# A three-batch GNN pipeline: every state and the neighbour sums take their turn through device memory, and the first norm moves

## The reference, cut to what matters

```python
adj_norm = adj / (jnp.sum(adj, axis=-1, keepdims=True) + EPS)
h_neigh = jnp.einsum('bnm,bmf->bnf', adj_norm, x)
h = relu(jnp.einsum('bnk,ko->bno', concat([x, h_neigh]), weight) + bias)
x = _layernorm(x + h)
...
A = (adj != 0).astype(x.dtype); h = x
for l in range(5):
    m = jnp.einsum('bnd,de->bne', h, weight[l])
    agg = jnp.einsum('bij,bid->bjd', A, m)
    h = _gru_cell(agg, h, w_ih, w_hh, b_ih, b_hh)
x = _layernorm(x + h * mask)
```

## Time and profile before

| what | value |
| --- | --- |
| median of 3 runs | 609.56 us (608.76 to 610.24) |
| the profiled execution, its own time | 608.95 us |
| its span, first to last instruction | 606.9 us |
| busy: TensorE, VectorE, ScalarE, GpSimd | 589.7, 513.5, 419.4, 419.4 us |
| mean granted TensorE clock | 0.992 |
| DMA: moved, share of the 16 engines | 73.55 MB, 37.7% |

### The profile page before, as it was taken

The page is one execution under the profiler, slowest core; times in us unless marked ns, Lnnn a source line. Parts: engine busy times, 40 slices in busy tenths (PEclk is TensorE's granted clock), DMA queues, the critical chain, the costliest instruction groups (busy, mean ns, idle before and its releaser), DMA issues.

```text
span 606.9 us, 9921 instructions
## 1 busy us (share of the span) xinstructions
PE 589.7 (97%) x2733; PEld 479.4 (79%) x2733; DVE 513.5 (85%) x1151; ACT 419.4 (69%) x777; POOL 419.4 (69%) x335
## 2 busy tenths in 40 slices
PE   7999999999999999999999999999999999999992
PEld 6678788888888888888888888888888888877771
DVE  5986969898998989899898989989898898966677
ACT  5767685958778595876868587685867768555451
POOL 0645464878868687886869688687977868755343
PEclk9999999999999999999999999999999999999996
DMA  8713122454344446334444534445453433010101
GB/s 271 294 35 114 54 76 88 134 180 121 123 151 112 161 127 190 121 121 146 115 154 138 190 112 130 141 115 158 138 174 110 148 138 95 10 53 10 44 0 53
DMA packets 74002, 73.55 MB, mean 121 GB/s; under 512 B 5760, under 2 KB 49280, under 8 KB 73984
## 3 DMA queue, kind: packets, MB, share of 16 engines
q1 hardware_dynamic: 73712, 73.20, 37.7%
q10 hardware_dynamic: 272, 0.13, 0.1%
HBM read 56.00 MB, written 17.30 MB: 121 GB/s over the span
## 4 chain that ended last, share of the span: by engine, by line
PE 91%; DVE 4%; DMA 1%; issue 1%; ACT 1%; SPq 1%; POOL 0%; POOLq 0%; DVEq 0%
PE ps_tok L1405 12%; PE ps_tok L1412 12%; PE ps_r L1269 6%; PE ps_r L1270 6%; PE ps_r L1271 6%; PE ps_z L1269 6%; PE ps_z L1271 6%; PE ps_z L1270 6%; PE ps_b L1271 3%; PE ps_b L1269 3%; PE ps_b L1270 3%; PE ps_in L1270 3%; PE ps_in L1271 3%; PE ps_hn L1271 3%; PE ps_in L1269 3%; PE ps_hn L1270 3%
## 5 line engine op out<-in xcount | busy, mean ns | idle before, releaser
L686 POOL TENSOR_TENSOR z_h<-z_gate,h 128x512 f32<-128x512 f32 x80 | 110.2, 1377 | 24.1 <-ACT z_gate L893 24.0
L676 POOL TENSOR_TENSOR h_lo<-h,h_hi 128x512 fp32r<-128x512 f32 x64 | 88.5, 1383 | 53.8 <-ACT h_hi L708 53.8
L811 ACT ACTIVATE ps_in<-ps_in,gru_bias 128x512 f32<-128x512 f32 x80 | 52.8, 660 | 53.6 <-DVE ps_in L1132 53.5
L1405 PE MATMUL ps_tok<-edges,tok_hi 128*128 (+1 forms) x320 | 87.8, 396 | 0.7 <-ACT tok_hi L708 0.7
L1412 PE MATMUL ps_tok<-edges,tok_lo 128*128 (+1 forms) x320 | 87.6, 396 | 0.0
L1248 DVE SCALAR_TENSOR_TENSOR r_hn<-ps_hn,gru_bias,r_gate 128x512 f32<-128x512 f32 x80 | 59.6, 745 | 28.1 <-ACT r_gate L883 26.9
L615 POOL TENSOR_TENSOR adjt_lo<-adjt_in,adjt_hi 128x512 fp32r<-128x512 f32 x56 | 72.1, 1312 | 4.3 <-ACT adjt_hi L708 4.3
L1405 PEld LDWEIGHTS ps_tok<-edges,tok_hi 128*128 128x128 f32 x320 | 59.7, 188 | 15.6 <-ACT tok_hi L708 0.9
L1412 PEld LDWEIGHTS ps_tok<-edges,tok_lo 128*128 128x128 f32 x320 | 59.9, 188 | 14.7 <-DVE tok_lo L919 0.3
L883 ACT ACTIVATE r_gate<-ps_r,rz_bias 128x512 f32<-128x512 f32 x80 | 55.2, 691 | 20.0 <-PE ps_r L1271 17.0
L1173 DVE SCALAR_TENSOR_TENSOR ps_in<-z_gate,ps_in 128x512 f32<-128x512 f32 x80 | 55.1, 689 | 10.9 <-ACT ps_in L811 8.6
(11 more groups left out here) (156 smaller groups left out, 1599.0 us busy)
## 6 DMA issues: line engine op xcount, KB each, us to landing
adjt_in<-in_adj_t_dram SPq DMA_DIRECT2D x14, 1024.0 KB, 5.4
adj_in<-in_adj_dram SPq DMA_DIRECT2D x14, 1024.0 KB, 5.3
rows<-passage SPq DMA_DIRECT2D x144, 64.0 KB, 2.0
passage<-early_blocks SPq DMA_DIRECT2D x24, 256.0 KB, 2.1
x_in<-in_x_dram SPq DMA_DIRECT2D x16, 256.0 KB, 3.8
xt_in<-in_x_t_dram SPq DMA_DIRECT2D x15, 256.0 KB, 3.0
out_dram<-y_out SPq DMA_DIRECT2D x15, 256.0 KB, 2.3
passage<-last_blocks SPq DMA_DIRECT2D x14, 256.0 KB, 2.1
```

The costliest lines, as they stand in the source:

```text
L676: nc.gpsimd.tensor_tensor(h_lo[new][:], h[new][:], raw(h_hi[new][:]), ALU.subtract).then_inc(s_h_lo, 1)
L686: nc.gpsimd.tensor_tensor(z_h[:], z_gate[:], h[own][:], ALU.mult).then_inc(s_zh, 1)
L1405: nc.tensor.matmul(ps_tok[:], tok_hi[:, c * P:(c + 1) * P], edges_from(c, unit[0]), start=c == 0, stop=False)
```

## The change

- **MOVED** takes slot 4 as well: state 3 goes through device memory (new `passage3`, `rows3`), and the TensorE turn between slots 3 and 4 goes.
- **Neighbour sums.** For windows 2 to 14 (`means`), VectorE transposes the 32x32 blocks of `ps_b[2]` in slot 1 into `late_blocks`, SyncE stores them to `mean_passage` and loads `mean_rows` with 4 DMAs. ScalarE's copy to `mean_t` and TensorE's turn in slot 2 go. `mean_parts` runs in slot 3 and adds into the banks `ps_b[0]` and `ps_b[1]`, where the products `own` now stay.
- **SyncE's queue.** Store 1, store means, load 1, load means, store 3, load 3, and then the adjacency loads.
- **Edges** are made in slot 0 and no longer in slot 2. The last batch's statistics move to slot 2.
- **First norm.** Residual and statistics in slot 3, moments in slot 4 ahead of `agg_lo`, and `norm1` behind `agg_lo`; `x1` is turned on TensorE between the z gate and the in gate of slot 4 (before: ahead of the r gate).
- **GpSimd** makes `tok_lo` for slot 4 (before: VectorE), and in slot 4 runs `z_h` ahead of the two `h_lo`.
- **Layer 0's state products** in the moved windows run their `h_lo` parts last (`first_state_products`), which wait for `s_h0_lo` alone.
- **ScalarE**: `xt_hi` goes from slot 0 to slot 4 of the window before, `x_kept` from slot 4 to slot 3; the scratch output of the row sums is `r_gate`.
- The wait for `s_agg_lo` stands directly ahead of the gates in every slot.

```diff
-MOVED = {slot: UNITS[slot][1] for slot in (1, 2, 3)}
+MOVED = {slot: UNITS[slot][1] for slot in (1, 2, 3, 4)}
...
+    def means(self):
+        return self.prepares() and not self.ramps()
...
                     store_state(w, 1)
+                if w.means():
+                    store_blocks(late_blocks, mean_passage, s_nsum_out, w.prepared(1, 1), s_mean_passed)
+                if w.trips():
                     load_state(w, 1)
+                if w.means():
+                    load_rows(mean_rows, mean_passage, s_mean_passed, w.passed(16, 1), s_mean_rows)
+                if w.trips():
+                    store_state(w, 3)
+                    load_state(w, 3)
...
-                        if slot == 2 and not w.ramps():
-                            if w.first >= 3:
-                                dve.wait_ge(s_agg, w.last_layers())
-                            edge_half(0)
+                        if slot == 2 and not w.ramps() and w.finishes():
+                            stats2_of_batch()
...
                         if slot == 0 and w.makes_parts():
+                            if not w.ramps():
+                                dve.wait_ge(s_adj_in, w.prepared(16, 16))
+                                if w.first >= 3:
+                                    dve.wait_ge(s_agg, w.last_layers())
+                                edge_half(0)
                             xw_parts(0)
+                            if not w.ramps():
+                                edge_half(1)
...
+                            if w.means():
+                                dve.wait_ge(s_nsum, w.prepared(1, 1))
+                                nc.vector.transpose(late_blocks[:]..., ps_b[2][:]...).then_inc(s_nsum_out, 1)
...
-                        if slot == 4 and not w.ramps():
-                            norm1(w)
+                        if w.means() and slot == 4:
+                            moments1(w)
...
-                        if slot == 2 and not w.leads():
+                        if slot == 2 and w.first == 1:
                             sums_by_tokens(w.prepared(1, 1))
...
-                    if unit:
+                    if unit and layer == 0 and w.first > 2:
+                        first_state_products()
+                    elif unit:
                         state_products(slot)
...
                         gate(ps_z, 1, agg_hi, agg_lo, wi_hi, wi_lo, False, True).then_inc(s_z_sum, 1)
+                        if slot == 4 and w.means():
+                            first_state()
```

More of the change, by code:

```diff
@@ L176, in blocks, with keeps, splits_next @@
         return 2 <= self.first < self.batches
+    def keeps(self):
+        return 3 <= self.first < self.batches
+    def splits_next(self):
+        return self.means() and self.first < self.batches - 2
     def last_made(self):
@@ L672, in window @@
                                                 tokens(raw(tok_hi[:])), ALU.subtract).then_inc(s_tok_lo, 1)
[L673 to L682, removed]
+                    if slot == 3 and w.first == 1:
+                        rstd1_of_batch()
+                    if w.unit_before(slot) and made < LAYERS and not (slot == 4 and w.means()):
+                        state_low(slot)
                     if w.unit(slot):
@@ L858, in window @@
                         evacuate(tok_hi[:], turned_bank(w)[:]).then_inc(s_tok_hi, 1)
-                    if w.unit_before(slot) and made < LAYERS and not (w.leads() or slot == 4 and w.first == 1):
+                    if w.unit_before(slot) and made < LAYERS and not (w.leads() or slot == 4 and (w.first == 1 or w.means())):
                         act.wait_ge(s_h, w.units(slot))
@@ L871, in window @@
                         y_hi_of(1, w.prepared(2, 2))
-                    if w.prepares() and slot == 4 and not w.ramps():
-                        h0_of_batch()
-                    if w.prepares() and slot == 1 and not w.leads():
+                    if slot == 1 and w.first == 1:
                         mean_t_of_batch()
@@ L882, in window @@
                             act.wait_ge(s_rhn, w.units(slot))
+                        if slot == 1 and w.prepares() and w.first > 0:
+                            act.wait_ge(s_row_sum, w.prepared(C, C))
                         nc.scalar.activation(r_gate[:], ps_r[:], ACT.Sigmoid, bias=rz_bias[:, 0:1]).then_inc(s_r, 1)
@@ L885, in window @@
                         x1_hi_of_batch()
-                    if w.prepares() and slot == 4 and not w.ramps():
-                        h0_hi_of_batch()
                     if w.unit(slot):
@@ L1188, in window @@
                     if w.prepares() and slot == 3 and not w.ramps():
[L1189 to L1190 removed]
+                        residual(w)
+                    if slot == 4 and w.means():
+                        norm1(w)
                     if slot == 4 and w.first == 1:
@@ L1195, in window @@
                         new_state(slot)
+                    if w.prepares() and slot == 3 and not w.ramps():
+                        stats1_of(w, range(C))
                     if w.starts_trip(slot):
```

175 lines of the change are left out of this document (114 added, 61 removed).

## The result

The changed kernel took 622.13 us (median of 6 runs, 619.3 to 623.68), the one before 608.93 beside it (6 runs, 608.37 to 610.24): a ratio of 1.0213, 95% interval 1.0188 to 1.0238. It is slower by 13 us where 5.6 us less was forecast. The profiled execution took 622.07 us, with a span of 620.3.

The account below looks back on a forecast made before the run. TensorE, busy 589.7 of 606.9 us, was taken as the bound: 11.0 us won from 25 turns, less 12 x (0.39 + 0.06) = 5.4 lost, leaves 5.6 won, so 604.0 us; range 600.5 to 608, chance 0.50.

Parts of the forecast that it names:

- TensorE's turns: State 3's and the sums' turns leave TensorE in the loop windows: 25 x 0.44 = 11.0 us won.
- The cost by starts: A turn on TensorE costs 0.44 us, counted between instruction starts, not four transposes of 275 ns in sequence.
- ScalarE and the trips through memory: ScalarE's changed copies, and state 3 and the sums going through memory, are hidden and cost nothing.
- GpSimd's chain into slot 1: GpSimd's operations from slot 4 to slot 1's `tok_lo` end at 8.68, so TensorE stalls 0.39 us a window.
- the second arrives (at about 8.2) when the last `tok_lo` is already running: Slot 0: the second `edges` does not delay GpSimd's chain, so two delays of 0.45 us count, not three.
- The same arithmetic gives `h_lo` of layer 0 at 2.9, against 3.2 for the first product that reads it: no stall: Slot 0: GpSimd's `h_lo` comes ahead of its first product on TensorE, so nothing is lost.
- VectorE's path: VectorE's lateness from slot 0 is worked off through slots 1 to 3; 0.06 us a window lost in slot 3.
- before, `pre2` fell between two GpSimd operations, and in my placing it still does, by 0.1 to 0.3 us: Slot 1: VectorE's `pre2` still avoids GpSimd's operations, with a margin of 0.1 to 0.3 us.
- VectorE is late by one GpSimd operation more: Rival: a wait at `pre2` in slot 1 or `var2` in slot 2 costs TensorE 0.9 us more; 614.8 us, chance 0.22.

Follow-up runs that it names:

- e6: Changed kernel with `pre2` moved whole to slot 2 behind `npre`, and `stats2` behind the new state: 620.44 us, ratio 1.0185.
- e9: Kernel before, with two idle 128x512 subtractions on GpSimd added around the `adjt_lo` operations of slot 1: 652.15 us, ratio 1.0719.
- e1: Changed kernel with the loop's `pre2` as one addition instead of four operations, node mask left out: 611.0 us, ratio 1.0033.
- e12: Changed kernel with the node mask moved to ScalarE and `pre2` as one addition, full computation: 611.24 us, ratio 1.0041.
- e8: Kernel before, with the loop's `pre2` as one addition, node mask left out: 608.84 us against 608.96, ratio 0.9997.
- e5: Changed kernel with `xt_lo` moved from VectorE's slot 0 to GpSimd at the end of slot 4: 606.07 us, ratio 0.9948.
- e4: Changed kernel with both `edges` operations back in slot 2: 628.26 us, ratio 1.0303.

## Why the prediction was wrong

**TensorE's turns: right.** 100 instructions fewer, and slots 2 and 3 without waits are 6.03, 0.44 us shorter than in the earlier trace rows. The cost by starts held, not the 275 ns each of the earlier trace rows.

**ScalarE and the trips through memory: right at nothing.** In the changed kernel TensorE waits for `tok_hi` once in the twelve windows, for 0.60 us at 138.46, in the first of them. The margin was real, as e6 shows: a transpose of state 3 that comes 0.7 us later makes `tok_lo` of slot 4 late.

**GpSimd's chain into slot 1: right in kind, too small.** I took two delays of 0.45 us on a chain ending at 7.78, so 8.68. There were three (`xt_lo` and both `edges`), and the chain started 0.26 later: 7.78 + 0.26 + 3 x 0.45 = 9.39. It ended at 9.40, and 0.76 us were lost, not 0.39. The step that failed is "the second arrives (at about 8.2) when the last `tok_lo` is already running": `edges` started at 7.33, 0.33 us ahead of `tok_lo`, and `tok_lo` took 1.74. The step before it failed too, "The same arithmetic gives `h_lo` of layer 0 at 2.9, against 3.2 for the first product that reads it: no stall". Done again, that arithmetic gives 2.74, or 2.84 with its 0.1 for a late operand. But I charged `xt_lo` to the chain's end and not to `h_lo`, which stood first in line behind it: with 0.45 it is 3.19, nothing to spare, and the chain began 0.26 late. It came at 3.49, and slot 0 lost 0.41. Together that is 0.78 us a window, 9 us.

**VectorE's path: wrong, and half of the miss.** The step is "before, `pre2` fell between two GpSimd operations, and in my placing it still does, by 0.1 to 0.3 us". It began 1.04 us ahead of the end of `adjt_lo` and let in three GpSimd operations: 4.12 us in place of 1.10. That made `agg_lo` late in slot 2 by 0.80 us, where I had 0.06 in slot 3. 12 x (0.78 + 0.74) = 18 us, the distance between 604.0 and 622.1; it comes out so closely because slot 2 lost nothing in two windows and slot 3 some 2 us in others. Both failures hang on the same meeting: I had the second `edges` wait for `tok_lo`, which puts `r_hn` at 9.2. Measured are 8.17 where `edges` went first, and 9.40 with a short `pre2` in the two windows where it waited. A margin of 0.1 to 0.3 us under a price of 3 us should not have been costed at nothing, all the less as slot 0 had uncertainties of 0.45 ahead of it.

**The rival** "VectorE is late by one GpSimd operation more" named the place, `pre2` in slot 1, and had the stall in slots 2 and 3 at 0.9 us (0.80 measured). It came out at 614.8 because it took GpSimd's part at 0.45. The page of the Trainium skill that it named (SBUF — State Buffer, Who interferes with whom) says that whoever starts first keeps the pair for the whole instruction; this case's traces agree, with 4.12 and 5.18 us for four operations of 0.28 each. That it gives no order for a queue of such operations left the price open; e9 shows one for one as long as GpSimd has its next operation ready, and in a gap of GpSimd's several VectorE operations go in a row.

Shown are the cause of slot 2's loss (e1 and e12 take it away, e9 makes such a loss in the other kernel, e8 excludes the operation's own length) and that of slot 0's (e5). For slot 1, e4 shows that without `edges` there is no wait; how much `xt_lo` adds is only read from the rows. That e5's `pre2` is short in all twelve windows still owes something to luck: nothing in the program holds `edges` behind `tok_lo`, or `pre2` in that gap.

## What to carry to other kernels

Where GpSimd and VectorE both work on operands in SBUF, count a run of small VectorE operations at one GpSimd operation each, whenever GpSimd has that many in its queue. Make such a run one operation, let another engine do a part, or hold it in a gap that GpSimd's own wait guarantees (the first two won time here, in e1 and e12; the third is an idea, and e6's move into such a gap won little). When a change shifts such an engine by tenths of a microsecond, who comes first at these meetings can decide more than the work that was saved: 11 us of TensorE work won here turned into 13 lost, and moving one operation of 0.68 us gave back 16.
